# Routing tables of a mixture-of-experts layer: the products in the rounded float format, high and low part apart

## The reference

```
x = x + mix(norm(x))            # 16-wide heads; softmax(sin(angle/2)^2) of the mean's Gram matrix, 1024 x 1024
x = x + ffn(norm(x))            # experts, see below
x = x + attention(norm(x))      # 16 heads of 64, causal
x = x + ffn(norm(x))            # the same expert weights again

def ffn(x):                     # n = 4 sequences, t = 1024 tokens, d = 256, e = 8 experts, f = 1024
    probs = softmax(x @ gate_w.T)            # per token over the 8 experts
    g, m = top_k(probs.transpose(0, 2, 1), k = 2 * t / e)     # each expert takes its 256 best tokens
    h = gelu(x[m] @ w1) @ w2
    out[m] += g * h
```

## Time and profile before

| | |
|---|---|
| runs of the kernel | 2151.43, 2155.18, 2152.21 us; median 2152.21 |
| the profiled execution | 2147.21 us, its span 2145.7 us |
| mean granted TensorE clock | 0.992 of full speed |
| TensorE busy | 2057.5 us (96%), 13666 products |
| VectorE busy | 1414.9 us (66%) |
| GpSimd busy | 1377.2 us (64%) |
| ScalarE busy | 904.7 us (42%) |

### The profile page before, as it was taken

How to read it: one execution, slowest core, us unless ns; L and a number is a source line. 1 busy time by engine, 2 the same in 40 slices (tenths; PEclk the granted TensorE clock), 3 DMA queues, 4 the chain that set the end, 5 groups by cost and what they waited for, 6 DMA issues and landing times.

```text
span 2145.7 us, 35631 instructions
## 1 busy us (share of the span) xinstructions
PE 2057.5 (96%) x13666; PEld 1598.7 (75%) x13666; DVE 1414.9 (66%) x3095; ACT 904.7 (42%) x1303; POOL 1377.2 (64%) x1238
## 2 busy tenths in 40 slices
PE   7998999999999999999999999999899999999998
PEld 5445888889786776767667766667666688899997
DVE  7375698585648667456766567874967646975554
ACT  6202553354334544335444244442444335444443
POOL 4313676677538877647778367753867937777774
PEclk9999999999999999999999999999999999999999
DMA  4533554556330001011110111101100245545552
GB/s 138 188 102 104 151 125 100 137 142 164 78 99 30 21 28 43 11 40 61 40 50 11 40 40 60 40 21 40 45 16 2 65 157 143 122 118 126 138 147 31
DMA packets 133785, 172.31 MB, mean 80 GB/s; under 512 B 16872, under 2 KB 109040, under 8 KB 133616
## 3 DMA queue, kind: packets, MB, share of 16 engines
q1 hardware_dynamic: 109040, 136.47, 20.0%
q0 software_dynamic: 24576, 33.57, 9.5%
HBM read 130.03 MB, written 39.85 MB: 79 GB/s over the span
## 4 chain that ended last, share of the span: by engine, by line
PE 67%; DVE 12%; POOL 6%; issue 4%; ACT 2%; DMA 1%; SPq 1%; POOLq 0%; DVEq 0%; ACTq 0%
PE psum L1406 12%; PE psum L1427 11%; PE psum L1576 9%; PE psum L1554 9%; PE psum L1477 7%; PE psum L1607 5%; PE psum L1491 4%; POOL t_acc L2598 3%; PE psum L1515 2%; PE psum L1592 2%; DVE psum L2331 2%; DVE f_hlo L2299 1%; DVE f_hhi L2297 1%; DVE t_mx L2362 1%; DVE f_wlo L2270 1%
## 5 line engine op out<-in xcount | busy, mean ns | idle before, releaser
L2598 POOL TENSOR_TENSOR t_acc<-t_acc,t_p 128x1024 f32<-128x1024 f32 (+2 forms) x254 | 416.8, 1647 | 21.3 <-POOL t_acc L2598 0.4
L1870 ACT ACTIVATE t_p<-psum 128x1024 f32<-128x1024 f32 (+2 forms) x291 | 292.4, 1019 | 85.3 <-PE psum L1554 76.0
L2515 POOL TENSOR_TENSOR f_wlo<-f_wst,f_whi 128x256 fp32r<-128x256 f32 x256 | 222.4, 946 | 164.3 <-ACT f_whi L1798 164.3
L1427 PE MATMUL psum<-f_whi,f_hhi 128*128 128x256 f32 x992 | 286.2, 289 | 8.6 <-DVE f_hlo L2299 8.5
L1427 PE MATMUL psum<-f_whi,f_hlo 128*128 128x256 f32 x992 | 280.3, 283 | 0.0
L1427 PE MATMUL psum<-f_wlo,f_hhi 128*128 128x256 f32 x992 | 280.1, 282 | 0.0
L2297 DVE CAST f_hhi<-f_h 128x512 fp32r<-128x512 f32 x256 | 140.6, 549 | 211.2 <-ACT f_h L1818 210.6
L1818 ACT ACTIVATE f_h<-psum 128x512 f32<-128x512 f32 x256 | 153.4, 600 | 282.7 <-PE psum L1406 269.7
L1576 PE MATMUL psum<-t_p,t_v 128*64 128x512 f32 (+3 forms) x1536 | 258.8, 486 | 1.5 <-POOL t_p L2578 1.5
L2612 POOL TENSOR_TENSOR t_yT<-t_pvs,t_den 128x512 f32<-128x512 f32 x64 | 84.3, 1317 | 260.0 <-ACT t_pvs L1880 230.9
L1576 PEld LDWEIGHTS psum<-t_p,t_v 128*64 128x64 f32 x1536 | 108.3, 137 | 162.3 <-issue 148.0
(11 more groups left out here) (307 smaller groups left out, 4669.2 us busy)
## 6 DMA issues: line engine op xcount, KB each, us to landing
f_wst<-in_L_ffn_w SPq DMA_DIRECT2D x64, 1024.0 KB, 5.8
t_wk<-wkT SPq DMA_DIRECT2D x32, 256.0 KB, 3.6
t_wq<-wqT SPq DMA_DIRECT2D x32, 256.0 KB, 3.8
t_wv<-wvT SPq DMA_DIRECT2D x16, 512.0 KB, 3.7
normal<-f_xy SPq DMA_DIRECT2D x5, 1024.0 KB, 5.4
a_x<-in_L_attn_a_x SPq DMA_DIRECT2D x4, 1024.0 KB, 7.5
res<-a_x SPq DMA_DIRECT2D x32, 128.0 KB, 2.7
t_xy<-res SPq DMA_DIRECT2D x4, 1024.0 KB, 6.3
```

The lines of the kernel that those rows point to most:

```text
L1427: m = pe.matmul(out, h[:, js], w[:, f, :], start=(f == 0 and a == 0 and j % 2 == 0), stop=(f == FT - 1 and a == 2), skip_group_check=True)
L1870: act.activation(t["group"][group], k.bank_pair[odd // 2][:, :, 0:k.group_width(group)], ACT.Exp, scale=1.0 / float(np.sqrt(k.DH))).then_i ...
L2515: m = pool.tensor_tensor(t["wlo"][n % 2][:, i, ks], t["wst"][:, i, ks], t["whi"][n % 2][:, i, ks].bitcast(F32), ALU.subtract)
L2598: pool.tensor_tensor(acc[:, :, q0:], (p0 if kt == 1 else acc)[:, :, q0:], p[:], ALU.add).then_inc(k.p_acc, 1)
```

## The change

- C, `hot` and A are written in the rounded format. Ones, zeros and token numbers are exact in it. The layout of C becomes (blocks, 2, experts, 16): all token columns, then all probability columns.
- The probabilities are split once per routing: `m1` = the probability rounded, `sel` = the probability minus that (two operations on 128 x 128 at the end of `positions`; marks "rounded" and "rest").
- `column` with c = 1 multiplies `hot` by the probability as before (the result is rounded on writing: the high part), and then once more in place by the rest (mark "C2"). For r = 0 this waits for GpSimd's token column, which reads `hot`.
- `table` does two passes per block with the same digits as weights: 256 columns (token and high part), then 128 columns (the low part from `hot`) onto the probabilities' half of the bank.
- In routing 2 the second sequence's `hot` waits until the first table has been computed; before it waited for the first sequence's products.
- `table_move` reads the bank in the new order and writes `Rw` in the old.
- The tiles' places in memory stay; they are only declared again in the rounded format.

```
         dve.tensor_scalar(t["lo4"][:], t["key"][:], 15, None, ALU.bitwise_and).then_inc(sem, 1)
+        dve.tensor_copy(t["m1"][:].bitcast(F32R), t["pr"][:]).then_inc(sem, 1)
+        self.after(r, "rounded")
+        dve.tensor_tensor(t["sel"][:], t["pr"][:], t["m1"][:], ALU.subtract).then_inc(sem, 1)
...
         if r == 2 and i:
-            self.after(r, ("C1", 0))
+            self.wait_filled(("table", r, 0))
...
-        dve.tensor_tensor(C[:, :, :, :, c], t["hot"][i], what, ALU.mult).then_inc(k.d_route.sem, 1 if r else 2)
+        hot = t["hot"][i]
+        dve.tensor_tensor(C[:, :, c], hot.bitcast(F32), what, ALU.mult).then_inc(k.d_route.sem, 1 if r else 2)
+        if c:
+            self.after(r, "rest")
+            if r == 0:
+                self.wait_ge(k.p_tokens, i + 1)
+            dve.tensor_tensor(hot, hot.bitcast(F32), spread(t["sel"][:, i], 3, 16),
+                              ALU.mult).then_inc(k.d_route.sem, 1)
...
-        self.wait_ge(k.d_route.sem, k.d_route.at(r, ("C1", i)))
-        C = t["C"][i]
+        self.wait_ge(k.d_route.sem, k.d_route.at(r, ("C2", i)))
+        C, rest, out = t["C"][i], t["hot"][i], k.bank[b][:, 0:k.E * 32]
+        probs = k.bank[b][:, k.E * 16:k.E * 32]
         for n in range(k.NBLK):
-            m = pe.matmul(k.bank[b][:, 0:k.E * 32], t["A"][i][:, n].rearrange("p e a -> p (e a)"),
-                          C[:, n].rearrange("p e c t -> p (e c t)"), start=(n == 0), stop=(n == k.NBLK - 1))
+            digits = t["A"][i][:, n].rearrange("p e a -> p (e a)")
+            pe.matmul(out, digits, C[:, n].rearrange("p t e c -> p (t e c)"), start=(n == 0), stop=False,
+                      skip_group_check=True)
+            m = pe.matmul(probs, digits, rest[:, n].rearrange("p e c -> p (e c)"), start=False,
+                          stop=(n == k.NBLK - 1), skip_group_check=True)
...
-        dve.tensor_tensor(t["Rw"], k.bank[bank][:, 0:k.E * 32].rearrange("p (e k) -> p e k", e=k.E),
-                          spread(k.same_f[:], 2, 32), ALU.mult).then_inc(k.drained[bank], 1)
+        dve.tensor_tensor(t["Rw"].rearrange("p e (k t) -> p e k t", t=2),
+                          k.bank[bank][:, 0:k.E * 32].rearrange("p (t e k) -> p e k t", t=2, e=k.E),
+                          spread(spread(k.same_f[:], 2, 16), 3, 2), ALU.mult).then_inc(k.drained[bank], 1)
```

More of the change, by code:

```diff
@@ L123, in semaphores @@
                              "Tfull", ("gt", 0), ("eq", 0), ("gt", 1), ("eq", 1), "m1", "pos1", "sel1", "sel", "pos",
-                             "key", "hi4", "lo4",
-                             *[(step, i) for i in range(2) for step in ("A", "hot", "C0", "C1")], ("R", 0), ("R", 1),
+                             "key", "hi4", "lo4", "rounded", "rest",
+                             *[(step, i) for i in range(2) for step in ("A", "hot", "C0", "C1", "C2")], ("R", 0),
+                             ("R", 1),
                              ("idx", 0), ("row", 0), ("idx", 1), ("row", 1))
@@ L189, in route_tiles, with rounded @@
         B, NBLK, D, E = self.B, self.NBLK, self.D, self.E
-        t["xy"] = [sb("f_xy", [P, NBLK, D]) for _ in range(2)][::-1]
+        def rounded(name, shape):
+            with ExitStack() as whole:
+                return self.sbuf(whole, name, shape, F32R)
+        t["C"], t["xy"] = [], []
+        for _ in range(2):
+            t["C"].insert(0, rounded("f_C", [P, NBLK, 2, E, 16])[:])
+            t["xy"].insert(0, sb("f_xy", [P, NBLK, D]))
+        hot, A = rounded("f_hotA", [P, 2, NBLK, E, 16])[:, 0], rounded("f_hotA", [P, 2, NBLK, E, 16])[:, 1]
         t["yT"] = sb("f_yT", [P, self.DT, self.L])
@@ L200, in route_tiles @@
             t[n] = sb("f_" + n, [P, 2, NBLK])
+        t["hot"] = [hot, rounded("f_hot", [P, NBLK, E, 16])[:]]
         t["wide"] = sb("f_wide", [P, NBLK, 2, E, self.NCAND])
@@ L208, in route_tiles @@
         t["ge"], t["need"] = sb("f_ge", [P, 2, 2, NBLK, E], BF16), sb("f_need", [P, 2, E])
-        t["A"] = [sb("f_A", [P, NBLK, E, 16])[:],
-                  t["yT"][:, 1, :].rearrange("p (n e a) -> p n e a", e=E, a=16)]
+        t["A"] = [sb("f_A", [P, NBLK, E, 16], F32R)[:], A]
         t["R"] = [sb("f_R", [P, 32]) for _ in range(2)]
@@ L215, in route_tiles @@
         t["gate"], t["gateT"] = sb("f_gate", [E, D]), sb("f_gateT", [P, self.DT, 32])
-        t["C"] = [xy[:].rearrange("p n (e k c) -> p n e k c", e=E, c=2) for xy in t["xy"]]
         t["pT"] = t["yT"][:, 0, :]
-        t["hot"] = [flat.rearrange("p (n e k) -> p n e k", n=NBLK, k=16)
-                    for flat in (t["pT"], t["wide"][:].rearrange("p n b e j -> p (n b e j)"))]
         return t
@@ L324, in early_tiles @@
             with ExitStack() as late:
-                lt = lambda n, s: self.sbuf(late, n, s)
+                lt = lambda n, s, d=F32R: self.sbuf(late, n, s, d)
                 t["A"] = [lt("e_A", [P, NBLK, E, 16])[:] for _ in range(2)]
                 t["hot"] = [lt("e_hot", [P, NBLK, E, 16])[:]] * 2
-                t["C"] = [lt("e_C", [P, NBLK, E, 16, 2])[:] for _ in range(2)]
-                t["Rw"], t["R"] = lt("e_Rw", [P, E, 32])[:], [lt("e_R", [P, 32]) for _ in range(2)]
+                t["C"] = [lt("e_C", [P, NBLK, 2, E, 16])[:] for _ in range(2)]
+                t["Rw"], t["R"] = lt("e_Rw", [P, E, 32], F32)[:], [lt("e_R", [P, 32], F32) for _ in range(2)]
             return
@@ L2495, in column @@
         self.wait_rows_moved(r, i)
-        pool.tensor_tensor(t["C"][i][:, :, :, :, 0], t["hot"][i], spread(spread(k.tokid[:], 2, k.E), 3, 16),
+        pool.tensor_tensor(t["C"][i][:, :, 0], t["hot"][i].bitcast(F32), spread(spread(k.tokid[:], 2, k.E), 3, 16),
                            ALU.mult).then_inc(k.p_tokens, 1)
```

## The result

Measured: 2163.62 us (median of 7 runs, 2158.49 to 2166.87) against 2153.22 us for the kernel before in the same session (7 runs, 2151.43 to 2156.96). The ratio is 1.0045, 95% interval 1.0031 to 1.0058: slower by 9.7 us (6.7 to 12.5). I had forecast 2151.7, within 2145.5 to 2157.

What follows compares the result with a forecast made beforehand. TensorE held two thirds of the chain of waits, but VectorE, SP or GpSimd decide at most tables. Routings 0 to 3, +2.8 - 2.5 + 1.0 - 1.8 = -0.5 us, gave 2151.7, range 2145.5 to 2157 (own range 2148 to 2155.5, chance 0.60).

Steps and rivals of the forecast that it cites:

- One table's cost: TensorE, each of 8 tables: 8 x 0.120 + 8 x 0.11 = 1.84 us instead of 3.45, 12.9 saved for eight.
- The 3.7 for the first table of routing 2: TensorE in routing 2: the new first table lies wholly at 1.2 GHz, 2 x 1.84 = 3.7 us instead of 5.39.
- Routing 0, +2.8: Before the first expert: VectorE's added work delays the stage 2.8 us, TensorE's shorter tables gain nothing; bounds 0 and +4.
- the chain that I named: Routing 0: VectorE's products and residual addition, SP's stores and sixteen table DMAs, indices, gather, then the first expert.
- Routing 2, +1.0: Attention's last units: rest product moves scores and GpSimd's sums by 1.14, both tables' savings are lost; +1.0 us.
- My bound of +4: Routing 2's upper bound: +4 us if both rest products are contended and show; the lower was -1.7.
- The signs that I had named: Routing 2: longer wait for GpSimd's mask at the attention's end; first table 1.7 shorter, yet the output product no earlier.
- Routing 3, -1.8: Two tables save 3.2 us, TensorE loses 1.4 standing still 0.9 and 0.5 for f_hlo; bounds -3.2 and 0.
- Routing 1, -2.5: Between experts: two tables save 3.2 us, less 0.4 for copy and subtraction and a 0.3 wait; bounds -3.2 and 0.
- VectorE's rest product decides, slower: Rival, chance 0.17: rest products beside GpSimd cost 1.76 to 2.3 us each, passed on whole; +7.3, 2159.5 us.
- TensorE's time carries: Rival, chance 0.17: f_hlo and rest products never hold TensorE in routings 1 and 3; -8.1, 2144.1 us.
- nothing at 128 columns: Rival, chance 0.06: low pass costs 0.216 each, a table 2.7, 3.2 us of routings 1 and 3 missing; +2.7, 2154.9.

Runs made afterwards that it cites:

- the second experiment: New tables in routings 1 and 3 only, routings 0 and 2 left float32, against the kernel before: 1.0004 (0.9995 to 1.0013), +0.9 us.
- VectorE's part alone: Kernel before, float32 tables, plus rounding copy, subtraction and rest products in all routings, results unread though tables still wait for them: 1.0059, +12.7 us.
- TensorE's part alone: New 256 + 128 column tables in all routings, without rounding copy, subtraction and rest product, against the kernel before: 0.9996 (0.9987 to 1.0004), -0.9 us.
- the fifth experiment: Rounded tables in all four routings, VectorE's copy, subtraction and rest product left out, against the kernel before: 0.9996, -0.9 us.
- VectorE held back: New tables in routing 2 alone, second sequence's one-hot products waiting until GpSimd's four sums end, against the kernel before: 1.0017 (1.0008 to 1.0027), +3.7 us.

## Why the prediction was wrong, point by point

- **One table's cost: right.** 0.23 us per block, 1.84 per table. The 3.7 for the first table of routing 2 was wrong: it ran at full clock, 1.84.
- **Routing 0, +2.8: right.** +2.9 at the first expert in the trace, +2.2 by the ratio, over the chain that I named.
- **Routing 2, +1.0: the step that failed most, +6.9 measured.** The path was right, the overlap wrong. I let GpSimd's sums move by the 1.14 us of VectorE's product and keep their length. I had the rows for better: 2.97 and 2.29 us for products beside GpSimd, and I used them for VectorE's side alone, never asking what a VectorE product does to a GpSimd sum. I also took the 1.7 us that TensorE's first table would save as lost and harmless; they moved VectorE's start onto the sums. 4.7 us of waits instead of 1, and the clock below 1 behind them, are the result. My bound of +4 was too near. The signs that I had named did come, TensorE's longer wait for the mask among them (3.54), but not their price.
- **Routing 3, -1.8: right.** -1.4 in the trace of the change, -1.5 in that of the second experiment, with the waits that I had named.
- **Routing 1, -2.5: the other step that failed.** With routing 3 it measured +0.9, so some +2.4 by itself; the traces of the changed kernel and of the second experiment give +2.5 and +3.4. Up to 377 us it went as forecast (-2.4 in the changed kernel, -1.8 in the second experiment), partly by luck: I had the second rest product end near 371.8, which is where the product ahead of it ends, and the wait of 0.3 that I drew from it was 0.26 and 0.85. I stopped the sum at the second table. VectorE's next instruction but a few waits for the table DMAs, and these depend on VectorE's `R`, not on TensorE: with 2.7 us more on VectorE they start 0.6 later while TensorE comes 1.8 sooner, so what TensorE gained turns into a pause 2.0 us longer and a lower clock behind it. Without VectorE's additions the pause takes the gain as well, so it is the wait in the queue and not only the added work. It was the chain of routing 0 once more, and I had read it there only.
- **The rival "VectorE's rest product decides, slower" (0.17, +7.3) came nearest** in sign and total: VectorE's part alone costs 12.7, TensorE's part alone brings 0.9. But much of that is luck. Its price wasn't met: five of the eight rest products took 1.21 or 1.22 us, two 1.76, one 3.36; and it too had neither the stretched sum nor the pause behind routing 1. "TensorE's time carries" is refuted by the fifth experiment, "nothing at 128 columns" by the table's 0.23 (its 3.2 us should have been four times 0.85, 3.4).
- **The range** was said to reach halfway to either rival. Halfway lie 2147.9 and 2155.6, my own inner range; 2145.5 to 2157 reaches further.
- **The price of lower clock** was in no term but that of routing 2's first table. The stretch 1684 to 1704 was granted 1.00 before, 0.74 after waits of 4.7 us, and 0.91 with VectorE held back and a wait of 2.10. How much of the 6.9 is the clock's I haven't separated: no run here keeps the waits and not the clock.

## What to carry to other kernels

Time taken from the engine that is 96% busy is worth only what the others let through: here 12.9 us of TensorE's gave 0.9, and 11 us of products put on VectorE at 66% cost 12.7. Follow a step past its last instruction to the next wait in the same engine's queue, above all one for a small DMA, and ask what is queued behind it. When an engine stops waiting earlier, look at what the engine that it can hold up was doing in that idle time, here GpSimd.

## What the runs showed of the hardware that I had not expected

- GpSimd's mask of 256 columns, 0.41 us alone, took 3.13 beside two VectorE products that kept their 1.21, and its 1024-column sum 4.58 for 2.36; elsewhere VectorE is the one stretched, its rest product 3.36 for 1.21 beside a sum and a mask.
- A rounded pass of 128 columns starts 0.17 us behind one of 256 with the same weights, and the next wide one 0.06 after it. My 0.12 + 0.11 had the right sum only.
- A product of VectorE writes every second word or contiguous words at the same price: 1.218 us before, and 1.22 after for the product of 370.74 with the token numbers. By the rule of the Trainium skill that the prediction weighed ("Vector Engine (DVE) Microarchitecture Reference", section "Measured stream behaviour on trn2") the old order should have been the slower one: the rows disagree.
- The table's drain, which now reads PSUM with a hop at every element, takes 0.41 us after, as the 0.416 of the earlier trace rows. VectorE's timeline after, routing 0:

```profile
174.32 0.41 DVE L2263 TENSOR_TENSOR f_junk<-psum,same_f 128x256 f32<-128x256 f32 x1
```
